# Exchange of attention probabilities through DRAM: loads cut by columns instead of partitions, tiles 0 and 1 included, short tiles' scores in two PSUM banks of their own

## Chip, cores and metric

The kernel runs on one core of a Trainium2 chip. The metric is the device time of one execution in microseconds (us), smaller is better. The time before is the median of three runs, and beside it stands one profiled execution.

## What is computed

Float32 throughout, a sequence of S = 1024 rows of D = 512 columns: a layer norm, causal attention with 32 query heads and 8 key/value heads of 128 columns each, an output projection, a layer norm and a residual; then a feed-forward block on block-quantised activations. Cut to the attention, with which the change deals:

```python
qkv = q @ w_qkv.T                     # 1024 x (4096 + 1024 + 1024)
scores = einsum('bskgd,btkd->bkgst', qh, kh) / sqrt(128)
scores = where(causal, scores, finfo.min)
probs = softmax(scores, axis=-1)
attn = einsum('bkgst,btkd->bskgd', probs, vh)
y = attn.reshape(1, 1024, 4096) @ w_dense.T
x = x + layernorm(y)                  # then x + layernorm(ffn(layernorm(x)))
```

## The kernel before

**Tiles.** The 8 key/value heads are 8 groups (G), each with 4 query heads (HG). A group has 8 tiles of 128 query rows. `TILES` (line 43) gives the tile index i of each of the 64 steps t; within a group the order is 3, 7, 2, 6, 1, 5, 0, 4 (line 40), and the last group ends otherwise. Tile i sees (i + 1) x 128 keys. Tiles 4 to 7 are long, tiles 0 to 3 short; each length has SBUF buffers of its own (`probs_long`, `squares_long`, `probs_short`, `squares_short`). A matmul on float32 data is three passes: every operand is split in a high and a low part (`hi`, `lo`), and the names of the trace show the parts.

**One tile.** `scores(t, u)` (line 1655) multiplies queries of head u with the keys into a score bank. `masked_max` (line 1295, instruction on line 1310) on VectorE (DVE) copies the scores out with the mask added and writes the negated row maximum `negmax`. ScalarE (ACT) does the exponential (line 1036), DVE the reciprocal of the sum (line 1317), GpSimd (POOL) or ACT the scaling (lines 722, 1042). The probabilities then have to be transposed before the product with the values, `weighted_values` (line 1703, matmuls on line 1719); `output_share` (line 1734) projects.

**Two ways to transpose.** A tile that is not `away(t)` is transposed on TensorE (PE) against the identity: `turn_probs` (line 1686, instruction on line 1700) into the two banks of `psT`, then `hi_of_turn` on ACT (line 1025) and `lo_of_turn` on DVE (line 1319). One such step is a "turn"; `HEADS` says which heads share one and `TURNS` lists them. A tile that is `away(t)` is exchanged through DRAM: `AWAY` (line 79) holds the steps 3 to 55, without tiles 0 and 1, which are `STAYING` (line 87). SP stores the rows of a pack (`PACKS`, line 80: all four heads for tiles 0 and 1, two packs of two heads for the others) into `p_scr` (`swap_away`, line 476, DMA on line 485), and loads them back (`swap_back`, line 487, four DMAs, issued on line 497). On the way the four blocks of 32 rows are exchanged with the four quarters of the columns, so that what remains is a transpose inside blocks of 32x32: `turn_squares` on DVE (line 1324, instruction on line 1329). Then ACT writes the high part (`hi_of_swap`, line 1031) and DVE or POOL the low part (`lo_of_swap`, lines 1331 and 724; `LOWS`, line 83, says which heads on which engine).

**Who waits for what.** A load waits for its pack's store and for the low parts of the previous tile of the same length, whose buffer it overwrites. A store waits for the scaling and, as there are two slots per pack in `p_scr`, for the load two tiles back. `masked_max` waits for the store of the tile two steps back. A score matmul waits until the maximum of the score two places earlier is done (`s_done`), since `psS` has two places for scores; `lane(t)` is 0 for every tile, so long and short tiles share them. `score_bank` (line 437) already knows a second lane, in `psT`.

**Order.** Each of the five instruction streams walks a written-out order: a string of letters (`SP_WEAVE`, `PE_WEAVE`, `ACT_WEAVE`, `DVE_WEAVE`, `POOL_WEAVE`, from line 157) names the kind of the next item and each kind has its own list. All transfers of the kernel are issued by SP.

The loads before, lines 496 to 499:

```python
for b in range(HG):
    sp.dma_start(rows[b * SPAN:(b + 1) * SPAN, :].rearrange("q (a x) -> q a x", a=HG),
                 p_scr[c][pack_count(t, k) % 2, k, :, b * w:(b + 1) * w].rearrange("(a q) x -> q a x", a=HG)
                 ).then_inc(swap_in[c][k], 16)
```

`rows` is 128 partitions by 4w elements, SPAN is 32, w a quarter of the pack's row. Each of the four DMAs writes 32 partitions, in each four pieces of w elements.

Of the kernel before, what the change touches and what calls it, by code (L numbers as in the profile page):

```python
# [20 lines left out]
def sandwich_kernel(nc, x, w_v, w_qk, w_dense, w_up, w_down, s_up, s_down, out):  # L21
# [129 lines left out]
    def woven(kinds, letters):  # L151
# [5 lines left out]
    SP_WEAVE = ("qqkqqwqoqoiioqqioiwoqqoiipqpjjqooipipqkjjqooiiqqooiioiqqoippwjqqjoopiijpqojqiokiqqooiiwqqoiopipjqjoqoipi"
             "qpojjoqiikqqooiioiqoqpijpwjqoqoipipqojjqioqqikooiiwoqqioipqpqjjooipiqpkqojjoiiqqooiioqqioippqjqjoqoipipq"
             "jojoiiqwkqqooiioqioiuqqqxq")
    PE_WEAVE = ("psppspssvvvvpspsspspypypvpvpsspvsspvsvvsyypspvssvssvyysyyvvpspssysyysysvvvvvvvssyyyvyvpssyyssyyvvvvvvssy"  # L160
             "yyyvssysyyssysssvvvvvssyyyssvvvsyvsssyyyyvvvvvvvvssyyyyvvvpsspssyysyysvvvvvvvssyyyvyvpssyyyysvsvvvvvssyy"
             "yyvssysysyysvsvssvvvssysvysvyvysvsssyyyyvvvvvvvvssyyyyvvvpsspssyyssyyvvvvvvvssvyyyyvpssyyyyssvvvvvvssyyy"
             "yvssysyyssyssvsvvvvssyysyvsvvysvsssyyyyvvvvvvvvssyyyyvvvpsspssyyysysvvvvvvvssyyvyyvpssyyyvssvvvvyvssyyyy"
             "vssyysysyssvvssvvvssvsysyvyvysvsssyyyyvvvvvvvvssyyyyvvvpsspssyyyyssvvvvvvvssyyyvyvpssyyysysvvvvvvssyyyyv"
             "ssyysysyssvvssvvsvssyyvsyyvvsvsssyyyyvvvvvvvvssyyyyvvvpsspssyyyyssvvvvvvvssvyyyyvpssyyyysvsvvvvvssyyyyvs"
             "syysysyssvvssvvvssvysysvyvsyvsssyyyyvvvvvvvvssyyyyvvvpspsyyssyyssvvvvvvvssvyyyyvpssyyysyvvvvvvssyyyyvssy"
             "yyyvsvvvvpspsyppyyyvvvvspspyyppyyppvspvvpsvvvvvppspsypyyvvyvsppssypyspyypsvpsvpvpsvvsvvppssyyyvyvpspspyp"
             "yypsypvpvpvvvvpsspsypypypypvpvpvvvpxyyyyvxxgxgyyyygxgxgxggdxdgdd")
    ACT_WEAVE = ("pppepqeeepopepqpqpepepqepeepneepnqpeepereorreeqehoeehepeeqqepoeeheohpeqeeqeohreeonheeeneeeqkkqoeeeheohnn"
             "eeqqkkereeoreeehoheeppeeeeqrqohheeoeepqeqeohreeonheeeneqekkeeoeenqehohneekeeqqkeoeheerrohpeeqqepeoeehrho"  # L170
             "rpqeeeeeeohqeeohneeeneqeeqkkeoeenehnohekekeeqqeoeheehoerrepepeeqqeohhoeereeerpeoqqheeohneeeneeeqkkeoeeqn"
             "ehoheenqqeeeekokeehoheeqpqerrreeeprohhoeeeqeeqepoheeonheeeneqeekkeeoenqheoheerneeqqrekekoeerhohpqqpeeree"
             "eeohheeopeeeqeqoheeonhqeeeneeekkeoqeqeenhnoheeeqkeeokeqheeoheerppeerqreoehhoeeperoqeeqhoeheeeeoppppoeppe"
             "pppqpqeppeepoppaepeqeoppepcppaeeqpieppcaeejoppceeeeiopipjppapepeppcaopepeipeppjpeppcaojpxicxojaixgjxgcia"
             "gxjcxgxtgigjtgxtdtgddtd")
    DVE_WEAVE = ("psppspssrrspspoppsprppsssprrsssprspsaprspsrosstrstasorsslsrlpstsaorrspstraosslsspartrotsslarosssurssaslr"
             "russkosstsstssroarlluaruskrsosrstratssolslsprssrtratopsslraossssrpartoslstarosslssrusarsusskrosrstsstssr"
             "oallusruastrkossrartssossllprpsrstoartssaosslrprssratoslstarosssursslsrussrakosrstssrtssaolluusraksrtosr"
             "strassosslplrssartprotssaolsrssrstpaorssltaorsslssrussarusskorsrstsstssraollsrurustarosskrtassolsslssrpa"
             "rptortssaoslsrsrmasprtossltroasslssrussurarssksorstsstssorallsrursukarosstrtassosllsrpssptrrtoassarolssr"  # L180
             "ssptaorssltraosslssrussaursrskosrstrsstssoalluusrsrkatosrstarossllsrspsrpastortssaoslsrastopssatorllssrs"
             "aopppspasrrosppppaspprppcssrppopsrpsrasopscsppdpssprspdapecpdsrsroppssfacrrpoepspppsaprcpdsepfsoppsppesp"
             "apdrprpcfodfpxaxecofexdgxgacfdegxfxgwxgewzfzgxwwzgzgwz")
    POOL_WEAVE = ("qnnnnqbnqqnnnnndnnnnqqnnlnnlqdnnrnnnnrqnnllnnqqnnnlrnrnnqqnknlnlnqnqnknrnnnrnnlldnnnnnnqqllnndnnnqnqnrln"
             "nnrqknnnqlnldqnqknnnnnnnlldqqnnnrnnnrlrlnnnnnqnqnlnqnnrnnkqnnlldqqknnnnnnnnllnnnqqnnrnrllnnnndnnqqrnrlnn"
             "nqknnnqlnlqqnndknnnnnnllqdrnnnrnnnqllnnnnrnqnqnlnqnnnrknnqlnlqqnnnnnknrnnlldnnnrqnnnqlnrlnrnndnnqqnlqnnn"
             "knnqnqnllnqnnknnqnnnllrrdnnnnnnqrllnnrdlnqunnnnnnnquunnqnnunyznqnqnuaynxnyqnnannanxnxynannnxyunnnnyaxawy"
             "xwaggxywgawgxgwgwgg")
# [36 lines left out]
    with ExitStack() as ctx:  # L225
# [237 lines left out]
        def _(sp):  # L463
# [1118 lines left out]
        def _(pe):  # L1582
# [72 lines left out]
            def scores(t, u):  # L1655
                n, e = keys_of(t, u), t // NT % 2
                if u == 0:
                    pe.wait_ge(q_lo, t + 1)
                    if t % NT <= 1:
                        pe.wait_ge(kv_lo, (t // NT) * PIECES_KV + 2)  # L1660
                if softmax_count(t, u) > 2:
                    pe.wait_ge(s_done[lane(t)], softmax_count(t, u) - 2)
                bank, queries = score_bank(t, u), [q[:, u * P:(u + 1) * P] for q in qT[t % 3]]

                def in_quarters(first, last, blocks, at_):

                    dst = bank[:, at_:at_ + (last - first) * SPAN * blocks].rearrange("p (c k x) -> p c k x", c=last - first,
                                                                                     x=SPAN)
                    shown = TILES[t] if first == 2 and u < 2 else blocks
                    return product(dst[:, :, 0:shown], [(queries, [k_[:, 0:blocks * P].rearrange(  # L1670
                        "p (k c x) -> p c k x", c=HG, x=SPAN)[:, first:last, 0:shown] for k_ in kT[e]])])

                if away(t) and n > BANK:
                    in_quarters(0, 2, TILES[t] + 1, BANK - n // 2)
                    last = in_quarters(2, HG, TILES[t] + 1, BANK)
                elif away(t):
                    last = in_quarters(0, HG, max(TILES[t] + 1, 2), 0)
                else:
                    at_, key = score_offset(n), 0
                    while key < n:  # L1680
                        cols = max(2 * P, min(BANK - (at_ + key) % BANK, n - key))
                        last = product(bank[:, at_ + key:at_ + key + cols], [(queries, [k_[:, key:key + cols] for k_ in kT[e]])])
                        key += cols
                last.then_inc(s_full[lane(t)], 1)

            def turn_probs(item):
                _, t, b, heads = item
# [192 lines left out]
```

## Time and profile before

| | us |
|---|---|
| runs, median of 3 (lowest, highest) | 1196.01 (1194.56, 1196.65) |
| the profiled execution, its own time | 1197.52 |
| its span, first to last instruction | 1195.7 |
| PE busy in the span | 1117.8 (93%) |
| DVE busy | 862.6 (72%) |
| POOL busy | 804.1 (67%) |
| ACT busy | 640.3 (54%) |

Busy time counts an instruction from its start to its end; register, branch, semaphore and DMA-issuing instructions do not count. The granted clock of TensorE was 0.983 of full speed on the mean of the span. The kernel's stages follow each other in time: projections up to about 250 us, attention up to about 880 us, feed-forward to the end; the exchange runs from 276 to 850 us.

### The profile page before, as it was taken

How to read it: one execution, taken by the hardware profiler on the slowest of the kernel's cores; microseconds unless marked ns; L12 is line 12 of the kernel's file. 1: busy time of each engine (PE TensorE's matmuls, PEld its weight loads, DVE VectorE, ACT ScalarE, POOL GpSimd, SP SyncE). 2: the span in 40 equal slices, each digit the busy share in tenths (PEclk: the TensorE clock that was granted, in tenths of full speed). 3: DMA queues.
4: the chain of work that ended last, by engine and by line, in shares of the span. 5: the costliest groups of instructions: out<-in, count | busy, mean ns of one | idle time of the engine just before them, and what ended most of it. 6: DMA issues, size and time to landing. Idle time of an engine off the chain costs nothing.

```text
span 1195.7 us, 16875 instructions
## 1 busy us (share of the span) xinstructions
PE 1117.8 (93%) x5218; PEld 928.2 (78%) x5218; DVE 862.6 (72%) x1698; ACT 640.3 (54%) x1237; POOL 804.1 (67%) x836
## 2 busy tenths in 40 slices
PE   8999999999989989989988989988899889999997
PEld 7888888888777767777767777867688768888885
DVE  4544546467788878788888878988667896666666
ACT  6432333258577665766766766755468642222224
POOL 7744457437859769677869579857585676656645
PEclk9999999999999999999999989989999999999999
DMA  6444664447899698797797795895430124333422
GB/s 216 137 179 145 190 211 141 143 139 221 255 270 266 200 286 250 219 301 212 257 280 235 242 286 171 265 304 150 128 98 1 53 56 146 94 116 114 119 66 94
DMA packets 157875, 216.89 MB, mean 181 GB/s; under 512 B 41056, under 2 KB 122592, under 8 KB 152928
## 3 DMA queue, kind: packets, MB, share of 16 engines
q1 hardware_dynamic: 157792, 215.89, 59.8%
q8 instruction: 40, 0.66, 0.2%
q14 instruction: 43, 0.35, 0.1%
HBM read 125.00 MB, written 90.83 MB: 181 GB/s over the span
## 4 chain that ended last, share of the span: by engine, by line
PE 54%; DMA 17%; DVE 13%; issue 5%; POOL 4%; ACT 3%; SPq 3%; DVEq 0%; POOLq 0%; ACTq 0%
PE psS L1586 16%; PE psOY L1586 14%; PE psT L1586 11%; DMA squares_long<-p_scr_long 10%; PE psOY L1719 7%; DMA p_scr_long<-probs_long 6%; PE psOY L1734 5%; DVE pT_lo L1242 4%; SPq L497 2%; DVE squares_long L1329 2%; PE psT L1700 2%; POOL pT_lo L662 1%; DVE probs_long L1310 1%; POOL probs_long L722 1%; DVE y L1387 1%
## 5 line engine op out<-in xcount | busy, mean ns | idle before, releaser
L1586 PE MATMUL psS<-kT_hi,qT_hi 128*128 128x384 f32 (+6 forms) x384 | 140.5, 366 | 40.6 <-DVE negmax L1310 40.3
L1329 DVE STREAM_TRANSPOSE squares_long<-squares_long 128x1792 f32<-128x1792 f32 (+3 forms) x54 | 102.2, 1893 | 62.9 <-DMA squares_long<-p_scr_long 62.9
L1036 ACT ACTIVATE probs_long<-probs_long,negmax 128x896 f32<-128x896 f32 (+9 forms) x124 | 122.4, 989 | 35.9 <-DVE negmax L1310 35.3
L722 POOL TENSOR_SCALAR probs_long<-probs_long,rsum 128x768 f32<-128x768 f32 (+9 forms) x98 | 93.2, 961 | 67.5 <-DVE rsum L1317 67.4
L662 POOL TENSOR_TENSOR pT_lo<-squares_long,pT_hi 128x896 fp32r<-128x896 f32 (+3 forms) x47 | 108.7, 2322 | 42.6 <-ACT pT_hi L1031 42.4
L1586 PE MATMUL psS<-kT_hi,qT_lo 128*128 128x384 f32 (+6 forms) x384 | 134.2, 349 | 0.0
L1586 PE MATMUL psS<-kT_lo,qT_hi 128*128 128x384 f32 (+6 forms) x384 | 134.0, 349 | 0.0
L1586 PEld LDWEIGHTS psS<-kT_hi,qT_hi 128*128 128x128 f32 x384 | 75.6, 197 | 58.1 <-issue 34.0
L1734 PE MATMUL psOY<-wd_hi,oT_hi 128*128 128x512 f32 x256 | 104.9, 410 | 10.1 <-DVE oT_lo L1242 8.7
L1031 ACT CAST pT_hi<-squares_long 128x1792 fp32r<-128x1792 f32 (+3 forms) x54 | 84.9, 1572 | 47.9 <-DVE squares_long L1329 47.6
L1242 DVE TENSOR_TENSOR pT_lo<-squares_long,pT_hi 128x896 fp32r<-128x896 f32 (+4 forms) x47 | 105.3, 2257 | 0.2 <-ACT pT_hi L1031 0.2
L789 POOL TENSOR_SCALAR hidden<-mask,hr,hs 128x128 f32<-128x128 f32 x112 | 50.1, 458 | 81.8 <-DVE hr L1407 81.8
L1734 PE MATMUL psOY<-wd_lo,oT_hi 128*128 128x512 f32 x256 | 101.6, 397 | 0.0
L662 POOL TENSOR_TENSOR qT_lo<-q_raw,qT_hi 128x512 fp32r<-128x512 f32 x64 | 89.4, 1402 | 17.5 <-ACT qT_hi L1020 17.4
L1734 PE MATMUL psOY<-wd_hi,oT_lo 128*128 128x512 f32 x256 | 101.0, 395 | 0.0
L1719 PE MATMUL psOY<-pT_hi,v_hi 128*128 128x512 f32 x222 | 89.8, 404 | 8.5 <-issue 4.2
L722 POOL TENSOR_SCALAR probs_short<-probs_short,rsum 128x512 f32<-128x512 f32 (+13 forms) x128 | 70.2, 559 | 35.7 <-DVE rsum L1317 35.6
L1586 PE MATMUL psS<-up_hi,xn1T_hi 128*128 128x512 f32 x224 | 87.8, 392 | 2.0 <-DVE mask L1400 1.0
L1078 ACT ACTIVATE mask<-psS 128x256 f32<-128x256 f32 x56 | 21.5, 384 | 123.0 <-PE psS L1586 123.0
L1719 PE MATMUL psOY<-pT_lo,v_hi 128*128 128x512 f32 x222 | 87.3, 393 | 0.0
L1586 PE MATMUL psS<-up_hi,xn1T_lo 128*128 128x512 f32 x224 | 87.3, 390 | 0.0
L1719 PE MATMUL psOY<-pT_hi,v_lo 128*128 128x512 f32 x222 | 87.3, 393 | 0.0
(208 smaller groups left out, 3282.6 us busy)
## 6 DMA issues: line engine op xcount, KB each, us to landing
q_raw<-q_scr SPq DMA_DIRECT2D x64, 256.0 KB, 5.3
p_scr_long<-probs_long SPq DMA_DIRECT2D x14, 896.0 KB, 6.3
squares_long<-p_scr_long SPq DMA_DIRECT2D x56, 224.0 KB, 5.7
p_scr_long<-probs_long SPq DMA_DIRECT2D x12, 1024.0 KB, 5.9
squares_long<-p_scr_long SPq DMA_DIRECT2D x48, 256.0 KB, 7.3
p_scr_long<-probs_long SPq DMA_DIRECT2D x14, 768.0 KB, 4.5
squares_long<-p_scr_long SPq DMA_DIRECT2D x56, 192.0 KB, 4.3
raw<-in_w_qk SPq DMA_DIRECT2D x10, 1024.0 KB, 6.4
```

The costliest lines, as they stand in the source:

```text
L497: sp.dma_start(rows[b * SPAN:(b + 1) * SPAN, :].rearrange("q (a x) -> q a x", a=HG), p_scr[c][pack_count(t, k) % 2, k, :, b * w:(b + 1) * ...
L662: return nc.gpsimd.tensor_tensor(dst, source, hi.bitcast(F32), ALU.subtract)
L722: nc.gpsimd.tensor_scalar(row, row, rsum[:, column(t, u)], 1.0, ALU.mult, ALU.mult).then_inc(p_ready[lane(t)], 1)
L789: last = nc.gpsimd.tensor_scalar(to, columns_of(h_sb[:, m % 2, b * P:(b + 1) * P], to), hr[:, m % 2, b:b + 1], hs[:, m % 2, b:b + 1], ALU. ...
L1031: nc.scalar.copy(turned_units(pT_of(t)[0], t, units), squared(t, units)).then_inc(swap_hi[length(t)], 1)
L1036: nc.scalar.activation(row, row, ACT.Exp, bias=negmax[:, column(t, u)], scale=-1.0, accum_out=lsum[:, column(t, u)]).then_inc(e_done[lane( ...
L1242: return nc.vector.tensor_tensor(dst, source, hi.bitcast(F32), ALU.subtract)
L1329: nc.vector.transpose(rows, rows).then_inc(swap_turned[c], 1)
L1586: last = nc.tensor.matmul(dst, a, b, start=(start and k == 0), stop=(stop and k == len(terms) - 1), skip_group_check=resumed)
L1700: last = nc.tensor.transpose(bank[:, k, j % TPB, :], whole_row(t, h)[:, j * P:(j + 1) * P], ident[:])
L1719: last = nc.tensor.matmul(psO, a, b, start=(j == 0 and k == 0), stop=(j == i and k == 2))
L1734: last = nc.tensor.matmul(psY, a, b, start=(h == 0 and k == 0), stop=(h == HG - 1 and k == 2))
```

## The change

Three things change, and with them the five orders.

- The four loads of a pack are cut by column quarters of the destination (a) instead of by blocks of 32 partitions (b): each writes all 128 partitions, w contiguous elements in each, and reads from DRAM the 32 rows of block a, all four quarters of each.
- `STAYING` is empty and `LOWS` has entries for tiles 0 and 1 (their low parts whole on DVE): in the steps 3 to 55 these tiles are exchanged too. Tile 0 has two turns instead of one where it still takes turns (`HEADS`).
- `lane(t)` is 1 for short exchanged tiles: their scores go to the two banks of `psT`, which turns use only in the steps 0 to 2 and 56 to 63. Two waits keep these uses apart: the first scores of the lane wait for the `FIRST_TURNS` turns of the steps 0 to 2, and the next two turns for the last short maximum.

```diff
-    LOWS = {0: (), 1: (), 2: (((0, 1), 0), ((2, 3), 1)), 3: (((0, 1), 0), ((2, 3), 1)), 4: (((0, 1), 0), ((2,), 0), ((3,), 1)), 5: (((0, 1), 0), ((2,), 1), ((3,), 1)), 6: (((0,), 0), ((1,), 1), ((2,), 0), ((3,), 1)), 7: (((0,), 0), ((1,), 1), ((2,), 0), ((3,), 1))}
+    LOWS = {2: (((0, 1), 0), ((2, 3), 1)), 3: (((0, 1), 0), ((2, 3), 1)), 4: (((0, 1), 0), ((2,), 0), ((3,), 1)), 5: (((0, 1), 0), ((2,), 1), ((3,), 1)), 6: (((0,), 0), ((1,), 1), ((2,), 0), ((3,), 1)), 7: (((0,), 0), ((1,), 1), ((2,), 0), ((3,), 1)), 0: (((0, 1, 2, 3), 0),), 1: (((0, 1, 2, 3), 0),)}
...
-    STAYING = (0, 1)
-    HEADS = {0: ((0, 1, 2, 3),), 1: ((0, 1), (2, 3)), 2: ((0,), (1,), (2,), (3,)), 3: ((0,), (1,), (2,), (3,)), 4: ((0,), (1,), (2,), (3,)), 5: ((0,), (1,), (2,), (3,)), 6: ((0,), (1,), (2,), (3,)), 7: ((0,), (1,), (2,), (3,))}
+    STAYING = ()
+    HEADS = {0: ((0, 1), (2, 3)), 1: ((0, 1), (2, 3)), 2: ((0,), (1,), (2,), (3,)), 3: ((0,), (1,), (2,), (3,)), 4: ((0,), (1,), (2,), (3,)), 5: ((0,), (1,), (2,), (3,)), 6: ((0,), (1,), (2,), (3,)), 7: ((0,), (1,), (2,), (3,))}
...
     def lane(t):
-        return 0
+        return int(away(t) and not length(t))
...
+    FIRST_TURNS = sum(item[0] < AWAY[0] for item in TURNS)
...
-    SP_WEAVE = ("qqkqqwqoqoiioqqioiwoqqoiipqpjjqooipipqkjjqooiiqqooiioiqqoippwjqqjoopiijpqojqiokiqqooiiwqqoiopipjqjoqoipi"
+    SP_WEAVE = ("qqwkqqqqoqoiipoqojiiqowpioqjiqpopjjqoiqipopkjqjqioiqpoqjoiiwpoqoqjpiiopjqjqoiqpipojoqjikipoqojiipqojowqi"
...
-                for b in range(HG):
-                    sp.dma_start(rows[b * SPAN:(b + 1) * SPAN, :].rearrange("q (a x) -> q a x", a=HG),
-                                 p_scr[c][pack_count(t, k) % 2, k, :, b * w:(b + 1) * w].rearrange("(a q) x -> q a x", a=HG)
-                                 ).then_inc(swap_in[c][k], 16)
+                for a in range(HG):
+                    sp.dma_start(rows[:, a * w:(a + 1) * w],
+                                 p_scr[c][pack_count(t, k) % 2, k, a * SPAN:(a + 1) * SPAN, 0:HG * w].rearrange(
+                                     "q (b x) -> b q x", b=HG)).then_inc(swap_in[c][k], 16)
...
                 if softmax_count(t, u) > 2:
                     pe.wait_ge(s_done[lane(t)], softmax_count(t, u) - 2)
+                elif lane(t):
+                    pe.wait_ge(t_done, FIRST_TURNS)
...
                 turn = TURN[item]
+                if FIRST_TURNS <= turn < FIRST_TURNS + 2 and SOFT[1]:
+                    pe.wait_ge(s_done[1], len(SOFT[1]))
```

## Rows read from the trace of the kernel before

**Rows 1.** Busy time of each engine in three stretches, granted clock, DMA share
```profile
core 0: us, PE busy (x) PEld busy (x) DVE busy (x) ACT busy (x) POOL busy (x), PEclk, DMA share, GB/s
0.00:275.00 275.00, 270.27 (x1248) 224.65 (x1249) 146.73 (x239) 113.27 (x209) 153.01 (x143) 1.00 0.53 168
275.00:850.00 575.00, 520.32 (x2425) 434.96 (x2423) 472.86 (x804) 379.03 (x691) 433.85 (x399) 0.97 0.83 246
850.00:1195.70 345.70, 327.19 (x1547) 268.63 (x1547) 243.05 (x657) 148.04 (x338) 217.22 (x295) 1.00 0.28 85
```

**Rows 2.** Waits between 262 and 860 us: total, times, longest
```profile
DVE squares_long L1329 <- DMA squares_long<-p_scr_long: 62.9, 37, 3.7
...
PE psS L1586 <- DVE negmax L1310: 39.3, 19, 4.7
```

**Rows 3.** The chain that ended last, shares of the span
```profile
PE 54%; DMA 17%; DVE 13%; issue 5%; POOL 4%; ACT 3%; SPq 3%; DVEq 0%; POOLq 0%; ACTq 0%
PE psS L1586 16%; PE psOY L1586 14%; PE psT L1586 11%; DMA squares_long<-p_scr_long 10%; PE psOY L1719 7%; DMA p_scr_long<-probs_long 6%; PE psOY L1734 5%; DVE pT_lo L1242 4%; SPq L497 2%; DVE squares_long L1329 2%; PE psT L1700 2%; POOL pT_lo L662 1%; DVE probs_long L1310 1%; POOL probs_long L722 1%; DVE y L1387 1%
```

**Rows 4.** DMA in windows 286:290 (exchange loads), 885:888.5 (loads of x), 345:356 (mixed)
```profile
GB/s 233 269 197 179 233 197 215 179 251 215 251 179 251 251 251 287 215 161 233 251 233 179 269 251 215 233 161 251 215 251 143 251 233 251 215 197 269 233 215 215
DMA packets 562, 0.90 MB, mean 225 GB/s; under 512 B 61, under 2 KB 562, under 8 KB 562
...
q1 hardware_dynamic: 562, 0.90, 108.0%
...
GB/s 375 375 375 351 351 398 375 398 398 375 351 421 351 351 374 375 375 398 375 304 398 304 351 281 258 328 281 281 281 257 281 328 351 304 351 375 375 421 398 351
DMA packets 672, 1.23 MB, mean 350 GB/s; under 512 B 74, under 2 KB 74, under 8 KB 672
...
q1 hardware_dynamic: 672, 1.23, 99.0%
...
GB/s 194 298 201 261 268 223 216 201 201 250 201 317 384 395 384 399 291 223 242 209 209 216 231 261 216 246 224 231 197 227 238 387 302 417 376 402 421 451 417 425
DMA packets 1468, 3.15 MB, mean 286 GB/s; under 512 B 160, under 2 KB 160, under 8 KB 1467
...
q1 hardware_dynamic: 1467, 3.13, 104.3%
```

**Rows 5.** One query load alone (893:898.5); then the exchange's loads, and their issue times
```profile
DMA packets 145, 0.28 MB, mean 51 GB/s; under 512 B 16, under 2 KB 16, under 8 KB 144
...
q_raw<-q_scr SPq DMA_DIRECT2D x1, 256.0 KB, 2.7
...
squares_long<-p_scr_long SPq DMA_DIRECT2D x56, 224.0 KB, 5.7
...
squares_long<-p_scr_long SPq DMA_DIRECT2D x48, 256.0 KB, 7.3
...
squares_long<-p_scr_long SPq DMA_DIRECT2D x56, 192.0 KB, 4.3
...
squares_long<-p_scr_long SPq DMA_DIRECT2D x56, 160.0 KB, 3.4
...
squares_short<-p_scr_short SPq DMA_DIRECT2D x48, 128.0 KB, 3.8
...
squares_short<-p_scr_short SPq DMA_DIRECT2D x48, 96.0 KB, 6.3
...
L497 SPq DMA_DIRECT2D squares_long<-p_scr_long x216: 302/432/1950, 280.5 to 843.7; - x108
```

**Rows 6.** Instruction groups between 262 and 860 us, shapes kept apart: PE, then DVE
```profile
L1700 PE MATMUL psT<-ident,probs_short 128*128 128x128 f32 x96 | 14.5, 272 | 0.0
...
L1329 DVE STREAM_TRANSPOSE squares_short<-squares_short 128x1024 f32<-128x1024 f32 x12 | 14.8, 1230 | 0.8 <-DMA squares_short<-p_scr_short 0.8
L1242 DVE TENSOR_TENSOR pT_short_lo<-psT,pT_short_hi 128x512 fp32r<-128x512 f32 x21 | 14.2, 674 | 1.5 <-ACT pT_short_hi L1025 1.4
...
L1329 DVE STREAM_TRANSPOSE squares_short<-squares_short 128x768 f32<-128x768 f32 x12 | 11.3, 953 | 0.0
L1242 DVE TENSOR_TENSOR pT_short_lo<-squares_short,pT_short_hi 128x1024 fp32r<-128x1024 f32 x6 | 10.3, 1712 | 0.0
...
L1242 DVE TENSOR_TENSOR pT_short_lo<-squares_short,pT_short_hi 128x768 fp32r<-128x768 f32 x6 | 8.1, 1356 | 0.0
...
L1310 DVE CUSTOM_DVE_ANT_0 probs_short<-psS,mask 128x256 f32<-128x256 f32 x7 | 2.9, 418 | 0.0
...
L1310 DVE CUSTOM_DVE_ANT_0 probs_short<-psS,mask 128x128 f32<-128x128 f32 x7 | 2.0, 280 | 0.2
```

More of the change, by code:

```diff
@@ L155, in woven @@
         return order
-    SP_WEAVE = ("qqkqqwqoqoiioqqioiwoqqoiipqpjjqooipipqkjjqooiiqqooiioiqqoippwjqqjoopiijpqojqiokiqqooiiwqqoiopipjqjoqoipi"
[L158 to L188, printed above, removed]
+    SP_WEAVE = ("qqwkqqqqoqoiipoqojiiqowpioqjiqpopjjqoiqipopkjqjqioiqpoqjoiiwpoqoqjpiiopjqjqoiqpipojoqjikipoqojiipqojowqi"
+             "qippojqqojipiojpkoqjiqpiojqopiqijoqwopqiijpoqjiopqiqkpojjioqipojqoiqiopowjiqipqojqpiqjopipoqjjkiopqiwoqj"
+             "oiqipqojoqipijpojqpiopiqoqjkjoiipojqqiopiqjooqiiuqxqqq")
@@ new lines, in sandwich_kernel @@
+    PE_WEAVE = ("pspsppssvvvvspspsyypspypypvpvpsspsvpspspvvbbvvbsbvbssyvyyyvvsbsbybyyysvvsvvvvvbsbsyyyvyvbbsyvsyyvvvvyvbs"
+             "sybyyybvbssyyyvvvvybvssbyyyyvvvvbbvvvvvyvvyyyvssybyvyvyvbssbbyyyyssvvvvvvvsbsbyvyyyvsbbvvbybyyvvyvvssysb"
+             "byyyvssyvvyyyvsvvsbbyyybvyvvvbssyvyvvyvvyvvvsbsyybyyvvvssbbvvyyvyvbyvvvbssbybvsyyyvbsbvvyyyyvvvvbssybyyy"
+             "vsbsybyyyvvvvvssyvyyyvbvvbssyyyyvvvvvvvbbvssbbyyyyvvvbsbsyyyyvvvvvvvbbssyyyvyvsbbvvyyyvvybvvsbyyyyvssvvv"
+             "yyyyvbvbssyyyyvvvvssbbyyyybvvvvvvvvssyyyyvvvsbsybybyyssvvvvvvvbsbsyyvyyvbbsvvvvyyyyvvbbsybyyyvssbbvbvyvy"
+             "yyvvssyyyyvvvvbsbsyyyybvvvvvvvvssyybvyyvvbbssyyyssyvvvvvvvbbssyvyyyvbbsybbyvvybyvvvvbsyyyyvbssvbvyvvyyby"
+             "vssyyyyvbsvvvssybyyyvvvvvvvvssyyvyybvvssbvvbyyvyyvvvvssyvsyyyvssyyyssyvvvvvvsyyyyvsyvvyvyyvvpspsyppyyyvv"
+             "vvpspsypypyypspvsppvsvvvvvvppsyppsyysyvvvpspsypypyypsvpsvpsvvpssvvvppssyyyyvvppsspyypyyppsvpvpvvvvppssyp"
+             "ypypypvvppvvvppyyxyyvxxgxgxyyyyxgggxggxdgddd")
@@ new lines, in sandwich_kernel @@
+    ACT_WEAVE = ("ppeppeqqeeoepperpepqpqpperpepepenpqpenfrfrqofefeeqehofhefqekfeofehhoffeqeqnffekeoqhfnefhoqekknffeqohehno"
+             "rffrrffkqkeeorqheeohqeeffffkqeeohhffeoenfffkfqeohhqenqeoekkffneeohnqhoeqeffffkkeeoqhrhorerffeffqekeohhqf"
+             "rfeffeoqnqeekohhnfeeoqfkfnfqkeeohhnoffeeffqkkeqeorffrfhrfheoekqeeqforfhhqfokeefnfeohheqfonfkfqekeohqeneh"
+             "onfrfrffeqekrokheeohqfffreqekfeeohhqffoeekffnqeohfhqfeonfqfeenkkohqeeohffnffkkeoeqheeorqhreqfferffekqeoh"
+             "hrffeoeqkffffenohhqeonffqeekknffohqeehofneqefrkkrroehrhefofeeqkfqfoeheqoheeeekohehoqeeoppeppeeopppqpepep"
+             "qpapeeceoppippejeqopepapecpipapeqpejcpeeiopeepejpoapepcpeppiappjecoppipepeppeppaopjpcxixjxagcogxixaxgjgc"
+             "xigtjggxdttgtddtd")
@@ new lines, in sandwich_kernel @@
+    DVE_WEAVE = ("pspspprsssrospspprppspparmsspspprspprbbbissbosisrtartboblsslbbsruisttioakrlsbbsaobibsrstiutkaborssbulalo"
+             "buirssbtaikotlrbblaobbusiiustkarosstlarbbossbblaruiissktrtolbbsisaorbubsbibtkatoisslrslbabouuksrsiatorbt"
+             "blssaolbrbsuiisuktaortlsslbobabbsisruitrkatbobsslbbuiasiotrstabkrbbossblulaoirssuktaoirtbbssauolblbsiris"
+             "uaktbrbobbitlisusoasrslrkbbttaiobsblsuosakbbrittauoslrblaobssiiuktroasstbabrloblbiuissatkuorsstrbaolbssb"
+             "blusiarsikrtotslbbsaouibrsbtitkabolbsulrabobissuritabobskstaolrbblsiisuuktaorssblbtraobsslubassiirtktorl"
+             "bbsiasobbruskbibtatiuobslrlbaobssbiurtkiaossbtraslbosluriukastotblsbslrosabrbiutiksaossrstaoslsruksstaot"
+             "rllaorsasoppprpassopspprpsarcppsspdpsorppssppesrfacopspdpprsascpserpsdppfrssopsseprrfacpospdppapscpeppdr"
+             "sfopspsprpparepcppdopfpxaecxfxdgogxacxxegfdgwxegfzgxwgzwzwzgwz")
@@ new lines, in sandwich_kernel @@
+    POOL_WEAVE = ("bnqnqnndnqndnqnnqnrmrmqrmmnnnnllnqnmmqmmnnlrlmqmnmmqnqlmqmnkmmqllnrdmmmrkqmnnqlnnldmmmmqnnqnnlmmlnmmqrqn"
+             "rlmqmnmmknlqldqmmmmnnknnlqlrrmmmmqnnnndqllmmmmnqqnrlnmmrqkqmmnldlmmmmnnqknqnrrmmmmllqnnnndmmlqlqmmnrrnlq"
+             "mmqmmknlqdnldmmqmmknnlnnrlrqqnmnmnmmnqllmnmmmqrrqlnmmqnmmklqdlnmmmmdknnlqnnqlrrmmmmqnnnnqlmmlnmmrrqmmqln"
+             "qmmkmmnlqdnlqmnmkndllrnnqmmrmmnnqrnnrllqnlununnnnunqnqzunnynnuanxnuqnnyqayxannnnnxnnnnqyaxnynnanxnnnyaxw"
+             "ywagwxgywagxggwgwgg")
```

## Prediction

> **What bounds the kernel now.** I read the busy time by stretch first. Before 275 us and after 850 us the tensor engine (PE) is busy 270.3 of 275.0 and 327.2 of 345.7 us and the DMA engines 0.53 and 0.28 of the time. Between them lies the attention, 575 us, and there three resources stand close together: PE is busy 520.3 us at a granted clock of 0.97, the vector engine (DVE) 472.9 us, and the 16 DMA engines 0.83 of the time at 246 GB/s [rows 1]. The change touches little outside this stretch. The waits in it come next: PE lost 39.3 us before score matmuls for the row maximum that frees a score bank, and DVE lost 62.9 us before its 32x32 transposes for the loads of the exchange [rows 2]. The chain that ended last agrees: PE has 54% of it, but the loads of the long tiles have 10% and the stores before them 6% [rows 3]. So the stretch is a ring (scores, softmax, store, load, transpose, values) with PE as its busiest member and the DMA engines a close second.
>
> How the loads move is the second reading. While nothing but them runs, at 286 to 290 us, all 16 engines are busy (108%: packets overlap a little) and yet only 225 GB/s move; loads into all 128 partitions reach 350 GB/s at 99% in rows of 2 KB, and 4 KB rows 417 to 451 GB/s [rows 4]. A load that writes 32 partitions thus takes some 1.6 times the engine time of one that writes 128. That is what the edit of the loads can save. The Trainium skill (SBUF — State Buffer, "Door 1: The DMA port swizzle") says that partitions 0 to 31 reach half of the 16 ports, 218 GB/s; the trace agrees, with 225.
>
> **The loads: what the new form gives up.** Today each of a pack's four loads has 32 partitions as the slowest dimension on both sides, with four pieces inside. A load by itself (256 KB of queries) shows 144 packets for 128 rows, 16 of them under 512 B: each of 16 engines adds one completion packet. The exchange's loads show the same share, 61 small among 562 [rows 4, 5]. So slowest dimensions of 128 and of 32 are dealt out over all 16 engines, in whole indices: 8 and 2 each. In the new form the destination counts 128 partitions, but the source pattern is "b q x", its slowest dimension the 4 quarters. If a transfer is dealt by whole indices of the slowest dimension, four indices cannot reach 16 engines: each load runs on 4; and if every load starts from the first engine, all loads of the kernel share the same 4. No row shows a pattern with a slowest dimension of 4, so both are inferences, and they decide the case. The Trainium skill (DMA: Bandwidth & Descriptors, "Why a DMA increments its semaphore by 16 and not by 1") states it as a rule: k is the largest number up to 16 that divides both slowest dimensions, on the lowest-numbered k engines, here 4. No run here shows that; the port rule of the other page would by itself make these loads faster.
>
> Its price. The loads move 56x224 + 48x256 + 56x192 + 56x160 KB for long tiles and 48x128 + 48x96 KB for short ones [rows 5], 55,296 KB or 56.6 MB. Seven tiles 0 (256 KB) and seven tiles 1 (512 KB) join: 5.5 MB, together 62.1 MB, of which each of four engines would take 15.5 MB. One engine's rate in full-speed rows is 350/16 = 21.9 GB/s (2 KB rows) to 451/16 = 28.2 GB/s (larger) [rows 4]; the exchange's rows are 0.5 to 2 KB, so I take 24, near the lower end because small rows are slower, raised a little for the overlap seen above. That is 647 us on each of the four, between 551 and 709. These engines also keep their sixteenth of everything else. All traffic takes 0.83 x 575 = 477 us of engine time [rows 1]; the present loads are 56.6 MB at 225 GB/s = 252 us of it, the rest 225 us. The new tiles' stores add 5.5 MB at 350 GB/s = 16 us. Sum 647 + 225 + 16 = 888 us of work on four engines in a stretch that lasts 575: it grows by 313 us, from +217 (at 551, never idle) to +400 (at 709 and about 3% idle). No cover is left: SP, which issues all transfers, is blocked behind its waits, DVE waits for the loads, and queries and weights queue in the same engines.
>
> **Tiles 0 and 1 exchanged.** 7x4 + 7x8 = 84 PE transposes go, at 14.5/96 = 0.151 us [rows 6]: 12.7 us of PE. Seven times, DVE loses three subtractions from PSUM (3 x 0.674) and gains a transpose of 1024 columns (1.230) and one of 512 (0.676, extrapolated from 1024 and 768), and a subtraction of 1024 columns (1.712) and of 512 (about 1.0, from 1.356 at 768). The maxima widen from an average 80 to 128 and 208 to 256 columns: about 0.5 us in eight. Sum +3.1 us, 22 us in all [rows 6]. ScalarE and GpSimd do the same copies and somewhat wider rows; they are busy 379 and 434 of 575 us, so I count nothing; with DVE waiting less, POOL would be next, still 140 us below the span. SP issues 14 stores and 56 loads more, 70 x 0.43 = 30 us [rows 5], in time that it now spends waiting; if it had none, the queries behind would be late by that.
>
> **Banks of their own.** Short tiles' scores go to the two banks that the PE transposes leave. A score there waits for the maximum two short scores back, no longer for a long tile's. At best all 39.3 us of waiting go [rows 2]; at worst none, since DVE must produce the same maxima at 82% busy. Two waits are new: the first short score waits for the first 16 turns (past by then), and turn 17, after the exchange, waits for the last short maximum, long done. Behind each PE would stop whole; I price both at nothing, at most one DVE step of 1.2 us each. All five orders are rewoven: the bound is that an engine meets one item too early per group, 7 x 1 to 3 us.
>
> **Sum.** The profiled execution took 1197.5 us (span 1195.7), 1.5 above the median. With four engines as the bound, PE's 12.7 and 39.3 us and DVE's 22 us all lie under the transfers, so they count nothing: 1197.5 + 313 = 1510.5, against the median 1509. Its own range is 1412 (+217) to 1600.
>
> **Rivals.** *All 16 engines carry the new loads* (faster). Loads take 62.1/350 = 177 us instead of 252, and the DMA share falls to (225 + 16 + 177)/575 = 0.73. PE then sets the stretch: 520.3 - 12.7 = 507.6 busy, DVE 472.9 + 22 = 495. Two engines this near each other leave some idleness; half of PE's 55 us idle recovered, less rounding for DVE, plus the 12.7 is a gain of 25, with 10 and 40 as ends: 1172, from 1156 to 1186. For it: the rows of 225 against 350 GB/s, which show a real waste. Against: nothing shows the slowest dimension of 4. It decides if one load leaves 144 packets. 0.24.
> *DVE becomes the bound* with 16 engines (slower, slightly): at the 0.82 duty that DVE holds now [rows 1], 495 us of work need 602, +27, less what shorter load waits return (say 12): 1211. 0.07.
> *It comes out even*: PE's saving and DVE's addition cancel, at 1196, within 2 us: 0.05.
> *Four engines carry the loads*, the forecast: 0.64. For it: the dealing by whole indices that 32 and 128 share, and an outermost 4 in the code. Against: no row of it. A gentler form, where each load takes another four engines so that four loads in flight cover 16, is counted in the first rival.
>
> **How the numbers follow.** About 0.2% is what a measurement of this kernel can tell from no change. Faster 0.24, within it 0.05, slower 0.71 (0.64 + 0.07). Cases of both signs hold the chance, so the range runs from most of the fast case to most of the slow one, 1162 to 1590, and leaves out about 0.15; the likeliest case alone is 1412 to 1600.
>
> **What would show it.** Right: each exchange load leaves 128 packets and 4 completion packets, not 16; mean DMA share falls toward 0.5 though the stretch is longer, GB/s near 100 while loads run alone; landing of long loads from 5 to 7 us now to over 10; DVE's wait for the loads grows to hundreds of us, PE's wait moves from the maximum to the low parts of the transposed probabilities; the clock falls oftener as PE idles. The steps of tiles 0 and 1: no PE transposes between 275 and 850 us, 14 more transposes of 512 and 1024 columns on DVE. Wrong: 16 completion packets a load and over 300 GB/s while loads run alone.

## The result, and the profile after

The changed kernel takes 1538.8 us in the median of four runs (1538.0 to 1540.3) against 1196.3 for the kernel before: a ratio of 1.286 (95% interval 1.284 to 1.289). The profiled execution has a span of 1537.4 us.

The busy time by stretch, columns as in [rows 1]:

```profile
core 0: us, PE busy (x) PEld busy (x) DVE busy (x) ACT busy (x) POOL busy (x), PEclk, DMA share, GB/s
0.00:275.00 275.00, 269.94 (x1242) 224.07 (x1242) 147.45 (x238) 111.54 (x206) 156.96 (x148) 1.00 0.52 168
275.00:1180.00 905.00, 583.62 (x2340) 479.23 (x2341) 460.30 (x813) 384.06 (x687) 427.32 (x379) 0.80 0.47 168
1180.00:1537.40 357.40, 333.19 (x1554) 272.94 (x1553) 243.11 (x656) 147.07 (x339) 213.73 (x295) 0.98 0.28 84
```

All but 12 us of the growth lies between 275 us and the end of the exchange: 905 us where [rows 1] have 575. DVE, ACT and POOL do no more work than before, and PE's busy time rises (583.6 against 520.3) although the transposes of the probabilities of tiles 0 and 1 are gone from it: its granted clock fell to 0.80 on average. The DMA share fell from 0.83 to 0.47 and the rate from 246 to 168 GB/s. So no compute engine is busy more than 64% of the stretch (PE), and the 16 DMA engines seem idle half the time. Why that is no room to spare is seen in a window with the exchange's loads and little else, 290 to 296 us:

```profile
GB/s 96 108 96 108 96 205 119 96 96 108 96 108 96 96 96 119 96 96 108 96 108 96 96 119 96 96 108 96 108 96 96 108 108 96 96 108 108 96 96 108
DMA packets 349, 0.62 MB, mean 104 GB/s; under 512 B 9, under 2 KB 348, under 8 KB 348
...
q1 hardware_dynamic: 348, 0.61, 26.2%
```

104 GB/s at 26.2% of 16 engines: four engines, busy all the time, 26 GB/s each. The 348 packets of the queue are 339 of data and 9 small ones, one small to 38 of data; before it was 61 in 562, one to 8 [rows 4]. With 128 packets of data to a load that is 3.4 completion packets a load, where there were 16. A window this short cuts loads at its edges; the count over the whole run, in the first experiment, gives exactly 4. The forecast's sign of the four engines is there in each number.

Waits between 275 and 1180 us, total, times, longest, beside [rows 2]:

```profile
DVE squares_long L1330 <- DMA squares_long<-p_scr_long: 329.1, 50, 11.8
...
PE psOY L1739 <- DVE oT_lo L1243: 193.0, 29, 12.2
...
ACT qT_hi L1021 <- DMA q_raw<-q_scr: 74.3, 17, 12.4
```

DVE's wait for the loads grew from 62.9 to 329.1 us. PE now waits before the output projection for the low part of the attention output (193 us): DVE stands before its transpose, waiting for a load, with that subtraction queued behind it. At 432 us, for example, DVE had waited 7.9 us for a load, and `oT_lo` was the fourth instruction behind the transpose. The query loads, unchanged themselves, come late too: they land in 8.0 us in the median instead of 5.3, and the stores of the long tiles' 896 KB in 12.1 instead of 6.3. Part of each has to go through the same four engines.

The chain that ended last, from the page:

```profile
PE 34%; SPq 26%; DMA 24%; DVE 7%; POOL 3%; issue 3%; ACT 2%; DVEq 0%; POOLq 0%; ACTq 0%
```

PE's share fell from 54% [rows 3] to 34%, and 26% is now SP's own queue, 3% before. The issue times of the loads say what that is (min/median/max in ns, first and last start in us):

```profile
L498 SPq DMA_DIRECT2D squares_long<-p_scr_long x216: 507/986/4304, 283.9 to 1172.0; - x108
L498 SPq DMA_DIRECT2D squares_short<-p_scr_short x152: 507/608/6172, 308.0 to 1156.0; - x152
```

A long tile's issue takes 986 ns in the median where it took 432 [rows 5], and some issues take over 4 us, one of a short tile 6.2. SP seems to be held until earlier transfers have moved on: eight issues in a row, of 192 KB each, took 14.05 us from 310.96 us on, 1.76 us each, and 192 KB at 104 GB/s take 1.9 us. That this is the reason was not tested by itself. Even the shortest issue of the new form took 507 ns, of the old one 302.

### The profile page after: what moved, and what is told of

Same layout as the page of the kernel before. It is cut to its first block, busy times and chain, and to the rows that moved or that the text cites. A ratio compares the mean times of both kernels' runs of the same rounds, so it can differ in the third digit from the quotient of the medians.

```text
span 1537.4 us, 16822 instructions
## 1 busy us (share of the span) xinstructions
PE 1186.7 (77%) x5134; PEld 976.2 (63%) x5134; DVE 850.9 (55%) x1706; ACT 642.7 (42%) x1231; POOL 798.0 (52%) x821
## 2 busy tenths in 40 slices
DMA packets 163538, 227.87 MB, mean 148 GB/s; under 512 B 37760, under 2 KB 126464, under 8 KB 158592
## 4 chain that ended last, share of the span: by engine, by line
PE 34%; SPq 26%; DMA 24%; DVE 7%; POOL 3%; issue 3%; ACT 2%; DVEq 0%; POOLq 0%; ACTq 0%
SPq L498 21%; DMA p_scr_long<-probs_long 12%; PE psOY L1587 11%; PE psS L1587 10%; PE psT L1587 8%; DMA p_scr_short<-probs_short 6%; DMA squares_long<-p_scr_long 4%; PE psOY L1739 2%; SPq L486 2%; SPq L475 2%; DMA squares_short<-p_scr_short 2%; PE psOY L1724 2%; DVE pT_lo L1243 1%; DVE y L1388 1%; PE psT L1705 1%
## 5 line engine op out<-in xcount | busy, mean ns | idle before, releaser
L1739 PE MATMUL psOY<-wd_hi,oT_hi 128*128 128x512 f32 x256 | 129.2, 505 | 223.1 <-DVE oT_lo L1243 205.7
L1739 PEld LDWEIGHTS psOY<-wd_hi,oT_hi 128*128 128x128 f32 x256 | 61.4, 240 | 246.6 <-DVE oT_lo L1243 236.0
L723 POOL TENSOR_SCALAR probs_short<-probs_short,rsum 128x256 f32<-128x256 f32 (+9 forms) x128 | 68.9, 551 | 131.8 <-DVE rsum L1318 131.7
L1587 PE MATMUL psS<-kT_hi,qT_hi 128*128 128x512 f32 (+5 forms) x280 | 106.3, 380 | 35.6 <-DVE negmax L1311 31.4
L1739 PE MATMUL psOY<-wd_lo,oT_hi 128*128 128x512 f32 x256 | 120.8, 472 | 0.0
L1739 PE MATMUL psOY<-wd_hi,oT_lo 128*128 128x512 f32 x256 | 119.5, 467 | 0.0
L1587 PE MATMUL psS<-kT_lo,qT_hi 128*128 128x512 f32 (+5 forms) x280 | 101.9, 364 | 0.0
L1587 PE MATMUL psS<-kT_hi,qT_lo 128*128 128x512 f32 (+5 forms) x280 | 101.4, 362 | 0.0
L1587 PE MATMUL psT<-kT_hi,qT_hi 128*128 128x256 f32 (+2 forms) x104 | 39.5, 380 | 72.2 <-DVE negmax L1311 72.0
L1037 ACT ACTIVATE probs_short<-probs_short,negmax 128x256 f32<-128x256 f32 (+9 forms) x128 | 70.2, 549 | 41.9 <-DVE negmax L1311 41.5
## 6 DMA issues: line engine op xcount, KB each, us to landing
p_scr_long<-probs_long SPq DMA_DIRECT2D x14, 896.0 KB, 12.1
```

What stands on the lines that cost most here:

```text
L723: nc.gpsimd.tensor_scalar(row, row, rsum[:, column(t, u)], 1.0, ALU.mult, ALU.mult).then_inc(p_ready[lane(t)], 1)
L1037: nc.scalar.activation(row, row, ACT.Exp, bias=negmax[:, column(t, u)], scale=-1.0, accum_out=lsum[:, column(t, u)]).then_inc(e_done[lane( ...
L1587: last = nc.tensor.matmul(dst, a, b, start=(start and k == 0), stop=(stop and k == len(terms) - 1), skip_group_check=resumed)
L1739: last = nc.tensor.matmul(psY, a, b, start=(h == 0 and k == 0), stop=(h == HG - 1 and k == 2))
```

## Experiments

Every experiment is compared with runs of the kernel before on the same chip (1194 to 1196 us in the median).

**The rest of the change without the new loads, and the new loads without the rest.** In the first the changed kernel gets the old loads back, in the second the kernel before gets the new ones:

```diff
-                for a in range(HG):
-                    sp.dma_start(rows[:, a * w:(a + 1) * w],
-                                 p_scr[c][pack_count(t, k) % 2, k, a * SPAN:(a + 1) * SPAN, 0:HG * w].rearrange(
-                                     "q (b x) -> b q x", b=HG)).then_inc(swap_in[c][k], 16)
+                for b in range(HG):
+                    sp.dma_start(rows[b * SPAN:(b + 1) * SPAN, :].rearrange("q (a x) -> q a x", a=HG),
+                                 p_scr[c][pack_count(t, k) % 2, k, :, b * w:(b + 1) * w].rearrange("(a q) x -> q a x", a=HG)
+                                 ).then_inc(swap_in[c][k], 16)
```

> The changed kernel with the old loads (each writes 32 partitions, slowest dimension 32); tiles 0 and 1 exchanged, the banks and all orders stay as changed. Theory (the four engines are the whole loss): 16 completion packets per load again, 225 GB/s while loads run alone, DMA share of the attention about (477 + 24 + 16)/575 = 0.90, and a time of 1180 to 1215 us, likeliest 1195, as PE's saving and DVE's and the DMA engines' addition cancel. Rival (the orders, the banks or the added exchange carry a good part of the loss): above 1250 us.

Measured: 1195.6 us, ratio 1.001 (0.999 to 1.003). A window with the loads alone, 288 to 292 us, and the stretch; then the packets of the whole run here, and of the whole run of the changed kernel:

```profile
DMA packets 558, 0.90 MB, mean 226 GB/s; under 512 B 62, under 2 KB 557, under 8 KB 557
...
275.00:850.00 575.00, 518.07 (x2374) 427.86 (x2374) 472.43 (x823) 385.95 (x694) 445.88 (x387) 0.98 0.92 266
...
DMA packets 167954, 227.89 MB, mean 191 GB/s; under 512 B 42176, under 2 KB 130880, under 8 KB 163008
...
DMA packets 163538, 227.87 MB, mean 148 GB/s; under 512 B 37760, under 2 KB 126464, under 8 KB 158592
```

62 small packets in 558 and 226 GB/s: the old form, and with it the whole loss is gone. The two runs move the same bytes, and the small packets differ by 42176 - 37760 = 4416. Each run issues 368 loads of the exchange, so it is exactly 12 small packets a load, 16 in the old form and 4 in the new. The DMA share of 0.92 is the 0.90 expected. The rest of the change is neither gain nor loss. Its waits show a trade, PE's between 262 and 860 us:

```profile
PE psOY L1739 <- DVE oT_lo L1243: 25.4, 19, 2.9
PE psT L1587 <- DVE negmax L1311: 11.2, 9, 3.6
PE psS L1587 <- DVE negmax L1311: 9.1, 9, 2.8
```

The 39.3 us of waiting for maxima [rows 2] came down to 20.3 with the added banks, and the wait for the low part of the output rose by 18 us, from 7.1: DVE was late at another of its items.

> The kernel before with the new loads alone. Theory (four engines carry the loads): 56.6 MB / 4 at the 26 GB/s that one engine showed in the changed kernel = 544 us, with the 225 us of the rest 769 us of work on four engines; at 96% busy 801 us instead of 575, so 1424 us (1390 to 1460), with 4 completion packets a load. Rival (orders and banks carry part of the loss): clearly under 1390 us. Rival (the old order suits slow loads worse than the new one): above 1460 us.

Measured: 1531.4 us, ratio 1.280 (1.276 to 1.285). The loads alone make the loss, but my sum was 107 us short, and the time lies in the case of the second rival, that the old order suits slow loads worse. The stretch, and the window 286 to 292 us:

```profile
275.00:1180.00 905.00, 597.20 (x2427) 488.14 (x2425) 463.04 (x804) 380.80 (x692) 437.51 (x400) 0.82 0.44 156
...
DMA packets 341, 0.62 MB, mean 103 GB/s; under 512 B 9, under 2 KB 339, under 8 KB 339
```

The rate of the loads is the same 103 GB/s. By the share, 0.44 x 905 = 398 us of 16 engines, of which the loads' 544 us on four engines are 136; so the four carried 544 + 262 = 806 us in 905, 89%. In the changed kernel the same sum is 597 + (425 - 149) = 873 of 905, 96%. With 5.5 MB less to load, the old order lets the four engines stand idle more often. Whether it is the added banks or the new orders that fill them in the changed kernel was not separated. The rest of the traffic, 262 us, was also 37 us more than the 225 of the sum.

**Two engines.** The new loads cut once more, so that the source's slowest dimension is 2 (the counts in `swap_in` doubled accordingly):

```diff
-                for a in range(HG):
-                    sp.dma_start(rows[:, a * w:(a + 1) * w],
+                for a in range(HG):
+                    for h in range(2):
+                        sp.dma_start(rows[h * 2 * SPAN:(h + 1) * 2 * SPAN, a * w:(a + 1) * w],
+                                     p_scr[c][pack_count(t, k) % 2, k, a * SPAN:(a + 1) * SPAN, h * 2 * w:(h + 1) * 2 * w
+                                              ].rearrange("q (b x) -> b q x", b=2)).then_inc(swap_in[c][k], 16)
```

> The changed kernel with each new load cut in two, of 64 partitions each, so that the slowest dimension of the source counts 2. Same bytes, same piece sizes. Theory (whole indices of the slowest dimension are dealt out, always from the first engine): 2 completion packets a load, about 52 GB/s while loads run alone, 62.1 MB / 2 at 26 GB/s = 1194 us on each of two engines and 276 us of the rest, at 96% busy 1531 us instead of 575: 2154 us in all (2050 to 2250). Rival (successive loads take other engines, and the loss is the latency of one load on few engines): eight loads in flight would then use 16 engines, and the time stays under 1600 us.

Measured: 2152.7 us (one run), and in the window 290 to 300 us:

```profile
DMA packets 291, 0.51 MB, mean 51 GB/s; under 512 B 8, under 2 KB 291, under 8 KB 291
...
q1 hardware_dynamic: 291, 0.51, 13.1%
```

13.1% of 16 engines is two, at 51 GB/s. The time is 1 us from the sum, which is luck in part: the sum's own range was 200 us wide. Over the whole run the small packets are 37760 again, as in the changed kernel, though the loads are twice as many: exactly 2 a load. This is the strongest evidence of the series: same bytes, same pieces, half the slowest dimension, half the engines. (Each load also writes 64 partitions instead of 128, and there are twice as many; old loads into 32 partitions ran at 225 GB/s, so fewer partitions are not what brings the rate to 51.) And loads issued one behind another do not spread over other engines, or eight of them would have filled all 16.

**New loads for the short tiles alone**, the old form for the long ones (`c` is 1 there), in the changed kernel and in the kernel before:

```diff
+                if c:
+                    for b in range(HG):
+                        sp.dma_start(rows[b * SPAN:(b + 1) * SPAN, :].rearrange("q (a x) -> q a x", a=HG),
...
+                else:
+                    for a in range(HG):
+                        sp.dma_start(rows[:, a * w:(a + 1) * w],
...
```

> The changed kernel with the new loads for the short tiles alone; long tiles are loaded in the old form. Theory (busy time on the most loaded engines sets the stretch): short loads 16.5 MB / 4 at 26 GB/s = 159 us, long loads 45.6 MB at 225 GB/s = 203 us, the rest 241 us: 603 us on four engines, at 96% busy 628 us instead of the 575 us of the run with all loads in the old form, so 1195 + 53 = 1248 us (1215 to 1275). Rival (a load on four engines hurts by its latency alone, and short tiles have slack): under 1210 us.

Measured: 1302.2 us, ratio 1.089 (1.086 to 1.092): 54 us above the sum and outside its range. Its stretch:

```profile
275.00:940.00 665.00, 532.09 (x2295) 436.98 (x2295) 465.08 (x801) 377.70 (x680) 425.99 (x376) 0.90 0.77 225
```

By the share, 0.77 x 665 = 512 us of 16 engines, of which the short loads' 159 us on four are 40; so the four carried 159 + 472 = 631 us in 665, 95%. They were as full as in the changed kernel. The 89% in the next expectation divides the 603 us of the sum by the stretch; the other traffic took 472 us and not the 444 summed. This run therefore does not show a cost beside that of full engines.

> The kernel before with the new loads for its short tiles (2 and 3) alone. Busy time on the four engines: short loads 11.0 MB / 4 at 26 GB/s = 106 us, long loads 203 us, the rest 225 us, together 534 us, less than the stretch of 575 us and than e8's 603. Theory A (only the busy time of the most loaded engines counts): no longer than 1210 us. Theory B (what the e8 run suggests, where four engines were busy 89% and the time 54 us above the sum: a load on four engines also lands later, and the ring of store, load and low part passes that on): 1220 to 1270 us.

Measured: 1254.9 us, ratio 1.053 (1.050 to 1.056). The sum of busy time on the four engines is below the stretch, and the kernel is still 5% slower: the time lies in theory B's range. The stretch (here 630 us), DVE's two transposes with the idle time before them, PE's first wait, SP's issues of the short loads, and the chain that ended last:

```profile
275.00:905.00 630.00, 539.00 (x2426) 446.70 (x2425) 471.98 (x805) 379.46 (x692) 431.54 (x399) 0.93 0.74 225
...
L1335 DVE STREAM_TRANSPOSE squares_long<-squares_long 128x1792 f32<-128x1792 f32 (+3 forms) x54 | 102.3, 1895 | 63.3 <-DMA squares_long<-p_scr_long 62.6
L1335 DVE STREAM_TRANSPOSE squares_short<-squares_short 128x1024 f32<-128x1024 f32 (+1 forms) x24 | 26.5, 1106 | 37.4 <-DMA squares_short<-p_scr_short 37.4
...
PE psS L1592 <- DVE negmax L1316: 64.4, 28, 5.9
...
L503 SPq DMA_DIRECT2D squares_short<-p_scr_short x96: 507/620/3870, 328.3 to 841.2; - x96
...
PE 49%; DMA 22%; DVE 10%; SPq 9%; POOL 4%; issue 4%; ACT 2%; DVEq 0%; POOLq 0%; ACTq 0%
```

The long tiles' wait is unchanged at 63 us; before the short tiles' transposes DVE now stands 37.4 us, against 0.8 in the kernel before [rows 6]. The written-out order puts the next maximum behind that transpose, and PE waits for it: 64.4 us where it was 39.3. PE's granted clock is 0.93 here against 0.97, and its busy time 539 us against 520.3, so some 19 of the 55 us by which the stretch grew are slower matmuls. By the share the four engines carried 106 + 440 = 546 us in 630, 87%. So on average they had time, and late transfers were paid for all the same. Which lateness it is stays open: the short loads themselves, the transfers behind them in the same engines (the stores of 1024 KB land in 9.8 us instead of 5.9), or SP, whose queue has 9% of the chain where it had 3%. An average also hides moments in which the four are full.

**128 partitions and 16 engines.** To have both, the reordering moves to the store. The scratch in DRAM is laid out in blocks (a, b, q, x); four stores each read 32 partitions, one load writes 128, and the slowest dimensions are 32 and 128 on both sides. The counts of `swap_out` and `swap_in` are changed with them.

```diff
-                sp.dma_start(p_scr[c][count % 2, k, :, 0:rows.shape[1]], rows).then_inc(swap_out[c][k], 16)
+                blocks = in_blocks(c, count % 2, k, rows.shape[1] // HG)
+                for a in range(HG):
+                    sp.dma_start(blocks[a].rearrange("b q x -> q b x"),
+                                 rows[a * SPAN:(a + 1) * SPAN, :].rearrange("q (b x) -> q b x", b=HG)
+                                 ).then_inc(swap_out[c][k], 16)
...
+                sp.dma_start(rows.rearrange("p (a x) -> p a x", a=HG),
+                             in_blocks(c, pack_count(t, k) % 2, k, w).rearrange("a b q x -> (b q) a x")
+                             ).then_inc(swap_in[c][k], 16)
```

> The kernel before, with the reordering moved to the stores: four stores per pack, each reading 32 partitions and writing DRAM in pieces of 0.5 to 2 KB (slowest dimension 32 on both sides), then a single load that writes all 128 partitions (slowest dimension 128 on both sides). As many DMAs as before. Theory (the number of engines and the partitions reached decide the rate): 16 engines in both directions; the load alone moves 330 to 400 GB/s instead of 225, and if reading 32 partitions is held to the same half of the rate as writing them, the stores fall to about 225 GB/s: a net change within 10 us of 1196. If reads are not so limited: 1175 to 1190 us. Rival (loads into 128 partitions are slow for another reason than the number of engines): above 1300 us.

Measured: 1189.8 us, ratio 0.995 (0.992 to 0.998). Windows 276.5 to 279 us (stores alone) and 286 to 290 us (loads, mostly):

```profile
GB/s 0 0 0 0 0 0 0 0 201 172 344 143 315 143 172 258 115 315 143 258 201 258 172 229 172 201 258 201 172 229 229 172 229 229 143 258 172 229 172 57
...
DMA packets 675, 1.20 MB, mean 299 GB/s; under 512 B 15, under 2 KB 674, under 8 KB 674
```

The load runs at 299 GB/s instead of 225. The stores move 0.41 MB in the 2.0 us in which the window is not empty, 205 GB/s. In the kernel before, the same window holds stores that read all 128 partitions:

```profile
GB/s 0 0 0 0 0 0 0 0 0 0 803 803 229 0 688 688 344 115 344 688 688 115 0 688 688 344 115 459 688 573 115 0 344 803 115 115 229 229 0 229
DMA packets 98, 0.70 MB, mean 281 GB/s; under 512 B 0, under 2 KB 0, under 8 KB 98
```

That is 0.70 MB in the 1.9 us from the first packet on, 373 GB/s. The turned stores differ from these in two things, 32 partitions and pieces under 2 KB instead of rows of 7 KB. The two were not separated, but pieces of the same size are no hindrance at 299 GB/s in the load, and the order of the stores matters (below); so reading 32 partitions is most likely held down as writing them is. The waste has moved from the load to the store, and the net is a gain of half a per cent.

> The changed kernel with the same turned stores and single 128-partition loads. Theory: the loss goes, within 15 us of the run that keeps the old loads (1180 to 1215 us), and 15 to 25 us below it if stores that read 32 partitions are not slowed. Rival (loads into 128 partitions are slow for another reason): above 1400 us.

Measured: 1190.5 us, ratio 0.996 (0.993 to 0.999); 5 us below the run with the old loads, not the 15 to 25 of the case in which stores are not slowed. Loads into 128 partitions are fast once 16 engines carry them; this rival of the four engines is out.

**The order of the four transfers.** Neighbouring blocks of 32 partitions (0 and 1) are issued one behind the other; in these four runs the order is 0, 2, 1, 3. The edit for the old loads (the second run has it in the loop of the turned stores, the last in the feed-forward's loads too):

```diff
-                for b in range(HG):
+                for b in (0, 2, 1, 3):
```

> The changed kernel with old loads (as e1_rest_only), the four loads of a pack issued in the order of blocks 0, 2, 1, 3, so that neighbouring loads lie in different halves of the partitions. Theory (neighbouring loads on an engine overlap little): unchanged within 3 us of 1195.5, 225 to 240 GB/s while loads run alone. Rival (engines that run ahead mix the halves): up to 300 GB/s and 1185 to 1191 us.

Measured: 1185.3 us, ratio 0.991 (0.989 to 0.994), while the run it differs from by this line had 1.001. The rival was right about the time, not about the rate: 242 GB/s at 288 to 292 us, where the run without this line had 226.

> As e4_turned_store_after, the four stores of a pack issued in the order of blocks 0, 2, 1, 3. Theory: the stores, at about 200 GB/s while they read one block of 32 partitions, stay so, and the time stays within 3 us of 1190.5. Rival (the halves mix): 1183 to 1187 us.

Measured: 1184.6 us, ratio 0.989 (0.987 to 0.991), against 0.996: the rival again.

> The kernel before, nothing changed but that the four loads of a pack are issued in the order of blocks 0, 2, 1, 3. By e7_loads_alternate against e1_rest_only (0.9%): 1184 to 1191 us if the gain comes from loads alone; 1192 to 1198 us if it needs the other parts of the change.

Measured: 1184.7 us, ratio 0.993 (0.991 to 0.996). One changed line in the kernel before gives the gain. Its issues, with KB and median us to landing, and DVE's transpose:

```profile
squares_long<-p_scr_long SPq DMA_DIRECT2D x56, 224.0 KB, 5.0
...
squares_long<-p_scr_long SPq DMA_DIRECT2D x48, 256.0 KB, 6.6
...
L1329 DVE STREAM_TRANSPOSE squares_long<-squares_long 128x1792 f32<-128x1792 f32 (+3 forms) x54 | 102.2, 1892 | 44.4 <-DMA squares_long<-p_scr_long 44.2
```

They land in 5.0 and 6.6 us instead of 5.7 and 7.3 [rows 5], and DVE waits 44.2 us for them, not 62.9 [rows 2]. In the window compared, 286 to 290 us, the rate rose only from 225 to 241 GB/s. How the engines share the halves of the partitions is not shown, nor that the halves are the reason: no other order, such as 0, 3, 1, 2 or 1, 0, 3, 2, was run.

> As e7_loads_alternate, with the same order for the loads of the feed-forward's hidden tiles (4 x 32 KB). Those run where the DMA engines are busy 0.28 of the time, so no port is crowded: within 3 us of e7's 1185 us. Rival (their landing shortens too): down to 1178 us.

Measured: 1182.4 us, ratio 0.991 (0.988 to 0.994): the same as without it, within the interval.

## Why the prediction was right

**The loads.** Both inferences held: the four indices of the slowest dimension go to four engines (26.2% of 16 busy), and always the same four (the run with two engines). The Trainium skill's rule (DMA: Bandwidth & Descriptors, "Why a DMA increments its semaphore by 16 and not by 1") thus agrees with the traces for k = 4 and k = 2: the whole runs show exactly 4 and 2 small packets a load, and 16 in the old form.

**The size.** 1509 us was forecast, 1538.8 measured, inside the case's own range of 1412 to 1600. The stretch was put at 888 us and is 905. Its terms were off both ways. The loads were taken at 24 GB/s an engine, 647 us; they run at 26, 597 us. The other traffic on each engine was put at 225 + 16 = 241 us and comes to 276 by the share (0.47 x 905 = 425, less the loads' 149). The sum, 873, is near 888; then the four engines idle for 4%, which the point left out. 12 us more lie behind the exchange. The mechanism was right, but that the point came within 30 us is partly luck: one term was 50 us too large, another 35 us too small. The same kind of sum, with the measured 26 GB/s, was 107 us short for the new loads alone. The upper rate of the range, 28.2 GB/s an engine from "4 KB rows", rests on one slice of a mixed window; between 354 and 355.9 us the 0.78 MB in 269 data packets average 2.9 KB a packet.

**Tiles 0 and 1, and the banks.** Priced at 12.7 us less of PE and 22 us more of DVE, both hidden, and at anything from nothing to 39.3 us of waiting. With the old loads all of it nets to 1.001, the case "it comes out even" of the first rivals; half the wait for maxima went and came back as a wait for the output's low part. The transposes are close to their prices: in the changed kernel seven of 512 columns took 697 ns each (676 assumed). The subtractions were cheaper, 1.430 us for 1024 columns (1.712 assumed) and 0.785 for 512 (about 1.0). In the run with old loads the rows of DVE's change sum to about 18 of the 22 us, yet DVE's busy time in the stretch stayed at 472.4 (472.9 before): the low parts of the long tiles, which nobody had priced, took 80 us there instead of 105. Why is not shown.

**The rivals.** "All 16 engines carry the new loads", forecast at 1172, can be read from the runs with turned stores only in part, since there the stores pay. It was too hopeful: a load at 299 GB/s and stores at 200 gave 1190. The first rival's premise, that loads into 32 partitions waste engine time, was right; a change of order alone is worth 9.5 us in the kernel before.

**The signs.** Four held: 4 completion packets a load, 104 GB/s with a DMA share of 0.47, DVE's wait in the hundreds, the granted clock from 0.97 to 0.80. One missed: PE's wait was to move to the low parts of the transposed probabilities, and it moved to the low part of the attention output (193 us), with 72 us still before maxima. One can't be read: the profile of the changed kernel gives no time to landing for these loads; that of the long tiles' stores rose from between 4.0 and 6.3 us to between 9.4 and 12.1.

**What the sum lacked** is that late transfers cost even where the four engines have time. It shows where they are not full: 1531 against 1424 summed for the new loads alone (89% busy), and 1255 where the sum gave no loss (87%). In the forecast case they were 96% busy and the term was small.

## What to carry to other kernels

Read a DMA's pattern for its slowest dimension on both sides before anything else: a form that reaches more partitions but puts a dimension of 4 outermost gave 104 GB/s for 225, on engines that everything else needs too. A mean DMA share is no measure of room; multiply the share in a window with one kind of transfer by 16 and count the engines, and compare the small packets of two whole runs, per transfer. Where transfers must write 32 partitions each, try the order 0, 2, 1, 3: it costs nothing and gave 0.7% to 0.9% here.

## What the runs showed that I had not expected

- An order of 0, 2, 1, 3 instead of 0, 1, 2, 3 in transfers of 32 partitions gained 0.7% to 0.9%, for loads and for stores. I had put it at nothing.
- Stores that read 32 partitions in pieces under 2 KB ran at 205 GB/s where whole stores ran at 373; loads that write 32 ran at 225.
- SP's issue of a load in the new form took up to 6.2 us, against at most 1.95 for the long tiles' loads before [rows 5]; 26% of the chain lay in SP's queue.
- The short tiles' loads, 11 of 217 MB, cost 5% when moved to four engines that were then busy 87% of the stretch.
